# Second expert layer of a two-layer block: tanh straight from PSUM for four of six pairs, down products one step earlier in TensorE's order

## The reference

```python
mag = jnp.einsum('td,ndh->tnh', fx, bank_mag)      # d = 128, h = 256, n = 16
freq = jnp.einsum('td,ndh->tnh', fx, bank_freq)
hidden = jnp.tanh(mag) * jnp.cos(jax.nn.softplus(freq) + 0.1 + bank_phase[None, :, :])
out_all = jnp.einsum('tnh,nhd->tnd', hidden, bank_down)
# each token takes its two best experts, weighted by a softmax, then an RMS norm
```

## Time and profile before

| | us |
|---|---|
| median of three runs (718.61 to 724.85) | 722.82 |
| the profiled execution | 708.11 |
| its span, first to last instruction | 706.3 |
| second expert layer: first ScalarE work of the layer to the last scatter | 565.45 to 683.90 |

### The profile page before, as it was taken

How to read it: one execution, slowest core, us unless ns; L and a number is a source line. 1 busy time by engine, 2 the same in 40 slices (tenths; PEclk the granted TensorE clock), 3 DMA queues, 4 the chain that set the end, 5 groups by cost and what they waited for, 6 DMA issues and landing times.

```text
span 706.3 us, 8174 instructions
## 1 busy us (share of the span) xinstructions
PE 449.7 (64%) x2119; PEld 303.1 (43%) x2119; DVE 477.1 (68%) x910; ACT 334.6 (47%) x652; POOL 412.9 (58%) x321
## 2 busy tenths in 40 slices
PE   3655976969787476634867788169540387886510
PEld 2322422423333232434766677025530287776410
DVE  5958899999899999870432233637733746866817
ACT  3165865673586264111222225276410079788705
POOL 0029999999899899216656664422475201753850
PEclk9887999999899799857899999569855589999765
DMA  5053556554344441014656674400012455553125
GB/s 185 0 181 106 188 173 191 185 163 155 120 148 153 135 146 63 15 33 146 196 169 189 189 215 131 119 0 1 15 49 67 164 184 180 186 191 117 42 76 143
DMA packets 58382, 90.21 MB, mean 128 GB/s; under 512 B 7569, under 2 KB 32658, under 8 KB 58338
## 3 DMA queue, kind: packets, MB, share of 16 engines
q1 hardware_dynamic: 52162, 78.88, 34.4%
q0 software_dynamic: 5024, 10.30, 4.7%
q10 hardware_dynamic: 1152, 0.52, 0.2%
HBM read 66.21 MB, written 11.14 MB: 110 GB/s over the span
## 4 chain that ended last, share of the span: by engine, by line
PE 18%; issue 10%; DVE 10%; POOL 7%; another core or an unknown queue 7%; DMA 3%; ACT 3%; SPq 2%; DVEq 0%; POOLq 0%; ACTq 0%
POOL y_dram L560 6%; PE ps L1266 5%; PE ps L1255 4%; PE ps L1306 2%; PE ps L1095 2%; PE ps L1424 1%; DVE ht L1857 1%; DMA y1b<-y_dram 1%; DMA xl<-h_dram,rows_i 1%; DVE ys L1867 1%; DMA y_dram<-ys,rows_i 1%; ACT h_tok L892 1%; SPq L512 1%; PE ps L1298 1%
## 5 line engine op out<-in xcount | busy, mean ns | idle before, releaser
L589 POOL TENSOR_TENSOR bu<-uT,b_sb 128x1024 f32<-128x1024 f32 x64 | 151.4, 2387 | 29.5 <-DVE uT L1769 29.5
L560 POOL DMA_INDIRECT y_dram<-ys,rows_i x86 | 92.2, 1072 | 112.2 <-DVE ys L2024 63.4
L1151 PE MATMUL ps<-prod,cst 128*128 128x512 f32 x256 | 127.0, 642 | 40.9 <-DVE yT L1803 16.4
L773 ACT ACTIVATE ps<-dtT,neg_a 128x512 f32<-128x512 f32 x128 | 83.2, 681 | 39.8 <-DVE prod L1793 27.3
L1151 PEld LDWEIGHTS ps<-prod,cst 128*128 128x128 f32 x256 | 49.9, 203 | 110.2 <-issue 74.6
L600 POOL TENSOR_TENSOR prod<-hs,c_sb 128x1024 f32<-128x1024 f32 x32 | 77.8, 2432 | 11.7 <-DVE hs L1783 5.9
L870 ACT ACTIVATE ht<-ps,b1T 128x128 f32<-128x128 f32 x78 | 24.4, 367 | 81.4 <-PE ps L1255 46.7
L1266 PE MATMUL ps<-w_s,ht 128*128 x312 | 47.0, 298 | 23.4 <-DVE ys L1867 14.1
L1266 PEld LDWEIGHTS ps<-w_s,ht 128*128 128x128 f32 x312 | 41.7, 208 | 28.0 <-issue 28.0
L551 POOL DMA_INDIRECT xl<-h_dram,rows_i x39 | 37.7, 966 | 26.9 <-DVE rows_i L1693 15.4
L1424 PE MATMUL ps<-xt,mfr 128*128 128x128 f32 x376 | 51.9, 294 | 1.8 <-issue 1.4
(11 more groups left out here) (289 smaller groups left out, 898.9 us busy)
## 6 DMA issues: line engine op xcount, KB each, us to landing
b_sb<-b_rows SPq DMA_DIRECT2D x32, 512.0 KB
c_sb<-b_rows SPq DMA_DIRECT2D x32, 512.0 KB, 4.1
mfr<-mf_s SPq DMA_DIRECT2D x47, 256.0 KB
w1r<-in_w SPq DMA_DIRECT2D x39, 256.0 KB
mf_s<-in_mf SPq DMA_DIRECT2D x16, 256.0 KB
xl<-x_slots SPq DMA_DIRECT2D x47, 64.0 KB, 2.0
w_s<-in_w SPq DMA_DIRECT2D x9, 256.0 KB, 4.6
down_s<-in_down SPq DMA_DIRECT2D x16, 128.0 KB
```

Source lines behind the costliest of these rows:

```text
L560: pool.indirect_dma_start(y_dram[l], bass.IndirectOffsetOnAxis(ap=rows_i[:, 1, j:j + 1], axis=0), ys[:, j % slots, :], None).then_inc(save ...
L589: nc.gpsimd.tensor_tensor(bu[:, g % RING, :, :], uT[:, c % 2, :, :], b_sb[:, k % BRING, g % 2, :].unsqueeze(1).broadcast_to([P, ND, CHUNK] ...
L773: nc.scalar.activation(decay_of(g, d), dtT[:, c % 2, d, :], ACT.Exp, scale=neg_a[:, d, n:n + 1]).then_inc(S["a_ready"], 1)
L1151: last = nc.tensor.matmul(bank(Y_BANK + d), ident, prod[:, g % RING, d, :], start=n == 0, stop=n == NS - 1)
```

## The change

Three things change, all in the second expert layer's main loop.

1. `mag_copy` applies Tanh instead of Copy for the pairs 0 to 3 of each quarter, straight from PSUM. `trig` then leaves out its Tanh for those pairs' groups (two of three); the third group is done as before.
2. ScalarE loads `SILU_TANH_SIN` ahead of the loop, and goes to `LOG_EXP` in step 3 of every quarter, the first one too, behind `mag_copy` of that step. The Exp and Ln of the first two groups follow it there together; until now the first group had them in step 2.
3. The down products are given out as 2, 2, 1, 1 over the steps 1 to 4 instead of 2 to 5. VectorE's `copy_y` moves with them, and `hidden` now stands right behind `take_up`.

```diff
+        def taken_by_tanh(p):
+            return p % QP < 4
...
-                                     ACT.Copy).then_inc(S["mag_sb1"], 1)
+                                     ACT.Tanh if taken_by_tanh(p) else ACT.Copy).then_inc(S["mag_sb1"], 1)
...
-                act.wait_ge(S["mag_sb1"], 2 * g + 2)
-                nc.scalar.activation(mag[:, group_slots(g), :], mag[:, group_slots(g), :], ACT.Tanh)
+                if not taken_by_tanh(2 * g):
+                    act.wait_ge(S["mag_sb1"], 2 * g + 2)
+                    nc.scalar.activation(mag[:, group_slots(g), :], mag[:, group_slots(g), :], ACT.Tanh)
...
+            act.preload_act_table_set(SILU_TANH_SIN)
             copy_xt1(0)
...
-                    if k and i == QG - 1:
+                    if i == 3:
                         act.preload_act_table_set(LOG_EXP)
-                    if i in (2, 3):
-                        softplus_tail(k * QG + i - 2)
+                        softplus_tail(k * QG)
+                        softplus_tail(k * QG + 1)
...
-                    if k and i in (2, 3):
-                        down_pair(d + 2 * i - 4)
-                        down_pair(d + 2 * i - 3)
-                    if k and i > 3:
-                        down_pair(d + i)
+                    if k and i in (1, 2):
+                        down_pair(d + 2 * i - 2)
+                        down_pair(d + 2 * i - 1)
+                    if k and i in (3, 4):
+                        down_pair(d + i + 1)
...
+                    if k and i < QG:
+                        hidden(g - QG + i)
+                    if k and i in (1, 2):
+                        copy_y(d + 2 * i - 2)
+                        copy_y(d + 2 * i - 1)
+                    if k and i in (3, 4):
+                        copy_y(d + i + 1)
```

More of the change, by code:

```diff
@@ L2031, in _ @@
                         turns(g - 1)
+                    if k and i < QG:
[5 more added lines that the diff above has]
+                        copy_y(d + i + 1)
                     if i == 3:
-                        if k:
-                            copy_y(d + 2)
-                            copy_y(d + 3)
                         argument(g)
@@ L2039, in _ @@
                         argument(g + 1)
-                        if k:
-                            copy_y(d + 4)
                     if i == 5:
                         turns(g + 1)
-                        if k:
-                            copy_y(d + 5)
                         argument(g + 2)
[L2047 to L2051, removed]
             turns(NG - 1)
```

## The result

| | before | after |
|---|---|---|
| median of 20 runs, us | 719.09 (707.32 to 731.24) | 724.29 (712.21 to 735.68) |
| ratio after to before | 1 | 1.0098, 95% interval 1.005 to 1.0145 |
| profiled execution, us | 708.11 | 715.76 |
| its span | 706.3 | 714.0 |

The change makes the kernel 1.0% slower, +7.0 us on 719.1 by the ratio (3.6 to 10.4 by its interval), +5.2 by the medians. The forecast was +4.1, its range -6.8 to +12.2.

The account below looks back on a forecast made before the run. ScalarE's late path and POOL's scatters were taken to bound the layer's end nearly evenly. Terms -3.7, outside idles +5.4 and clock +2.4 summed to +4.1, giving 726.9 us on a median of 722.8; range 716 to 735.

Parts of the forecast that it names:

- Tanh from PSUM costs what the copy costs: ScalarE's magnitude instructions: 596 ns each, no change, bounds -0.06 and +0.06; two group Tanhs fewer gain 1.9 us a quarter.
- The new order puts `hid1` on the path: TensorE's step 1: down products wait for `hidden`, holding back step 2's up products; ScalarE waits 3.0, later another 0.6 us.
- T+4.6: End of VectorE's `hidden` of the first group, 4.6 us after the quarter's first Abs on ScalarE; nothing in the change moves it.
- 24.25 us a quarter without outside idles: ScalarE's quarter under the new order: work falls to 19.9 us, but 4.3 of waiting on TensorE come in.
- outside idles: Idle times without a late semaphore: 3.6 us a quarter before, half counted, 1.8 three times, +5.4; bounds 0 and 10.8.
- The clock term: TensorE's down products slow after idling: +1.6 us at each of three places, half taken, +2.4; bounds 0 and 4.8.
- The first quarter: ScalarE's new switch to `LOG_EXP` there adds 1.5 us, bounds 1.3 and 1.9; the load ahead of the loop is free.
- The end: First copy of the final down products at 665.5, 3.2 us sooner; POOL's scatters are through earlier and idle for it.
- T+7: Start of POOL's run of scatters in quarter 3, about 7 us after the quarter's first Abs, at 643.
- The 0.5 for POOL's backlog: POOL's last scatters: it already stands idle for the final copy, so the end comes 0.5 us sooner still.
- the -3.7: Whole layer, outside idles and clock left out: 3.2 us sooner at the final copy and 0.5 at POOL.

Follow-up runs that it names:

- series 1: One chip, kernel before 719.0 us: changed kernel with old order 713.74; before with new order alone 721.13; changed kernel with `hidden` first 725.23, with 20 transposes 721.96.
- series 2: Another chip, kernel before 678.7 us: changed kernel with cut weight loads 683.55, with first quarter undone 688.0; the same two with old order 673.18 and 674.86.
- series 3: Third chip, kernel before 717.9 us: changed kernel 723.14; kernel before again 715.56; Tanh and switches with old order 713.35; changed kernel with `hidden` first and 12 transposes 724.86.
- the two profiles of series 2: Changed kernel with its first quarter as before, 688.0 us, ratio 1.0244, and the same with the old order, 674.86, ratio 1.0026.
- the clean chip: Chip whose four profiles showed no outside idle of 1 us or more on ScalarE in quarters 1 to 3; kernel before 678.7 us.
- small loads: Changed kernel with weight loads from pair 4 on cut from 512 columns to 64: 683.55 us, ratio 1.012; same with old order 673.18, ratio 1.0015.
- the first-quarter kernel: Changed kernel with its first quarter as before, no Tanh from PSUM or switch there: 688.0 us, ratio 1.0244; same with old order 674.86, ratio 1.0026.
- The filling with transposes: Changed kernel with 20 identity transposes on TensorE ahead of each quarter's first down product: 721.96 us, ratio 1.0052.

## Why the prediction was right

Right in sign and mechanism; that the number came so close is partly luck, as the last points show. By its own steps:

- **Tanh from PSUM costs what the copy costs.** 594 against 596 ns. Right. That it is a gain with the old order, together with the late switch: 0.990 and 0.991 of before in series 1 and 3. In series 2 no gain is shown.
- **The new order puts `hid1` on the path.** Shown by taking it away (+9.8 us in medians of series 3, 723.14 against 713.35; 10.4 and 13.1 in series 2) and by the waits. `hidden` ended at T+4.6 (591.18 - 586.61), as worked out from the earlier trace rows. Taking the order back also moves VectorE's copies; that the price lies in the steps with the wait is read from the two profiles of series 2.
- **24.25 us a quarter without outside idles.** Seen on the clean chip. Where the products stayed fast, in quarter 1 with small loads, it was 24.9. In quarter 2 of the first-quarter kernel it was 26.8, with the clock's loss in it (3.15 and 2.52 instead of twice 1.95, so 1.8): 24.25 + 1.8 = 26.05. So 0.7 is left in either. The term was sized well.
- **The clock term,** 1.6 at half of three places. Mis-sized: the products were slow in all three quarters in the profile after, 2.75, 3.78 and 3.78, and so was the up pair behind them, which the sum had left out (2.92, 2.66 and 2.17). Over 1.95 apiece that is 6.4 us and not 2.4, more than the upper bound of 4.8. The filling with transposes shows the cause.
- **The first quarter,** 1.5 with bounds of 1.3 and 1.9. From its first Abs to quarter 1's: 585.93 - 568.02 = 17.9 before, 586.61 - 565.87 = 20.7 after, 2.8 more. The first two Abs, before and then after:

```profile
568.02 0.60 ACT L986 ACTIVATE fabs<-ps 128x512 f32<-128x512 f32 x1 [1.76 <-PE ps L1424]
...
570.43 0.60 ACT L986 ACTIVATE fabs<-ps 128x512 f32<-128x512 f32 x1
```

```profile
565.87 0.60 ACT L990 ACTIVATE fabs<-ps 128x512 f32<-128x512 f32 x1 [1.76 <-PE ps L1430]
...
569.28 0.60 ACT L990 ACTIVATE fabs<-ps 128x512 f32<-128x512 f32 x1 [0.41 <-PE ps L1430]
```

  Of the 2.8, 1.0 lies between these two (3.41 against 2.41), where the change touches nothing; in series 1 and 3 this distance was 2.0 to 3.2, and 2.0 and 3.0 in the two kernels with the quarter as before. What the change added is 1.8: the switch, and 0.51 of waiting for the turned rows of step 3, which the first group's Exp and Ln had filled. That is inside the bounds. On the chip of series 2 it cost nothing, since there the turned rows set the pace.
- **The end.** POOL's run of quarter 3 started at T+7.6 (T+7 predicted) and its last eleven scatters stood idle for 4.30; that scatters which come sooner are worth nothing while the last copy sets the end, holds. The 0.5 for POOL's backlog came too: POOL now follows the first copy's end by 678.03 - 677.75 = 0.28 us and not by 0.8.
- **Outside idles,** half of 3.6, so 1.8 a quarter. The layers of the two profiles differ by 9.9 us (565.45 to 683.90 before, 563.30 to 691.64 after). How much of that is outside idles, one profile of each can't say. That these idles are no property of the kernel is the reading that fits the chip without them, where kernels with either order had none; a fixed share of them was a guess that the median can't test. It is here that luck comes in: of the sum's terms the -3.7 and the clock's 6.4 alone give +2.7, and with 0.7 more for each of three quarters +4.8, against 7.0 measured. So about 2 us, an estimate, are left for the outside idles where the sum had 5.4. The clock was put too low and the outside idles, by this, too high, and the two errors cancelled in part.
- **No adding up.** Implied by the sum and not said: by the medians the same new order costs 2.1 us with Tanh as before (series 1, 721.13 against 719.02) and 9.8 with Tanh from PSUM (series 3). The difference, 7.7, fits a gain of the other part (4.5 to 5.3 us by itself) made worthless, but the intervals are as wide as it. What shows it are the waits, longer by the 1.9 us of the Tanhs saved.

The version that beats the kernel before in series 1 and both kernels in series 3 is the one with Tanh from PSUM, the late switch and the old order. In series 2 its nearest relative, with the first quarter as before, beat the new order and equalled the kernel before.

## What to carry to other kernels

When an engine works in order, ask of each step that is moved ahead not what waits for it but what stands behind its wait. The down products gained a place nobody needed (their scatters had slack until the last batch) and took it from up products that ScalarE needs at once. And before work is taken off an engine, look whether the same change makes that engine wait: then the saving only lengthens the wait.

## What the runs showed of the hardware

- In the changed kernel a wait of 2.95 to 4.95 us on TensorE was followed by two down pairs at 1.4 to 1.9 times their duration (2.75 to 3.78 us against 1.95), with a granted clock of 0.50 in one such stretch. Not every wait did it: after one of 2.58 us with small loads they took 2.05. 20 small transposes in the wait kept them at 2.05 in all three quarters.
- The same kernel took 719.0, 678.7 and 717.9 us (medians) in three series on three chips. On the middle one the idle times without a late semaphore, single ones of up to 8.13 us elsewhere, were absent from ScalarE in this layer. They can't be the whole of the 40 us: the layer began at 529 to 540 us there and at 562 to 577 on the others, so 22 us or more were gained ahead of it. The cause of the idles and of the difference stays open: cutting the loads was tried only on the chip that had none.
- A table switch within this layer took 1.28 us with the next activation at most 0.02 later in every profile (586.16 to 587.46 in the first-quarter kernel with the new order), except once, 0.50 later, in the kernel with Tanh and the switches alone. The Trainium skill, page "ScalarE: Activation LUTs", section "What ACT_TABLE_LOAD costs", adds a drain of 1.38 us to each. No switch here shows it, and the measurement decides.
